# Maximum of the scores ahead of the output add and the rotation sum on VectorE, in a fused FFN, attention and FFN kernel

## The chip, the cores and the metric

One core of a Trainium2 chip runs the whole program. The metric is the device time of one execution in microseconds (us), taken as the median of several executions. The engines are TensorE (PE in the profile, with its weight loads as PEld), VectorE (DVE), ScalarE (ACT), GpSimd (POOL) and SyncE (SP, which here only issues DMAs).

## What is computed

The reference is a "macaron" block in fp32 over x of shape 2 x 1024 x 256: half a mixture-of-experts FFN, causal attention with rotary positions, and the same half FFN again.

```
x = x + 0.5 * ffn(layernorm(x))
x = x + attn(layernorm(x))
x = x + 0.5 * ffn(layernorm(x))

attn: q, k, v = x @ wq, x @ wk, x @ wv        16 heads of 128
      q, k = rope(q), rope(k)
      logits = q k^T / sqrt(128), masked causally
      probs = softmax(logits)
      out = (probs @ v) @ wo
```

The FFN has 8 experts that differ by low-rank parts, with a top-2 router; it does not matter to the change.

## The kernel before

Three stages follow each other: the first FFN, the attention, the second FFN. The change is in the attention alone.

Precision: a product of two fp32 operands is made of three TensorE matmuls in a fast fp32 form, on high and low parts (`product`, lines 1241 to 1245). So each operand has to be split: ScalarE copies the high part (`..._h`), and VectorE or GpSimd subtracts it from the original for the low part (`..._l`, the helper `low` at line 295).

Attention: heads are taken in 8 pairs. A pair has four units (2 heads x 2 sequences), a unit has 8 query tiles of 128 rows, and each tile is one **step**, so `STEPS` is 32 per pair. Step t works on tile i = t % 8 of its unit; its scores are 128 x 128(i+1) elements wide. Every engine runs its own written-out list of instructions, step by step, and semaphores join them. Work of several tiles is in flight: the tile of step t is transposed at step t + 2 (`T_LAG`), its probabilities meet the values at t + 5 (`PV_LAG`, two tiles at a time), the output projection is at t + 8 (`OUT_LAG`).

What a step does, for each engine in its order of issue:

- TensorE: `scores` of tile t; the side work (`project`, a 128 x 512 piece of q or k of the unit after, in even steps, or `values` in odd ones); `weigh` (probabilities times values, even steps); `project_out` (odd steps of the even units); `turn` (transposes of tile t - 2).
- ScalarE: copies of the transposed tile t - 3 (`pT_h`, line 768); in even steps `rope_high` (line 750), the high part of the piece of q or k of step t - 2, which waits for VectorE's sum; in odd steps `oA_h` or `oB_h` and the values' high part; then `Exp` of tile t (line 789), which waits for the maximum; in even steps `swap_halves` (lines 744 and 745, two copies), which waits for VectorE's `rope_cos`.
- VectorE: the order that is changed, below; then `pT_l` of tile t - 3; `rope_cos` (line 1110, even steps) or `value_low`; the low part of the output; reciprocals of the row sums (line 1129).
- GpSimd: the scaling of tile t - 1 by its reciprocal (line 571), `rope_sin` (line 560), the low part of the piece of step t - 2.

The three instructions that change places on VectorE are these. The **output add** (line 1162) adds a 128 x 512 tile of the output projection, which TensorE has made at step t - 1, to x; it comes in even steps, in 8 of a pair's 32 (t = 2, 4, 6, 8, 18, 20, 22, 24; in the first pair only the last four). The **rotation sum** (line 1116) ends the rotation of the piece of q or k that was projected at step t - 2; it comes in all even steps for which there is such a piece. The **maximum** (line 1173) reads the scores from PSUM in place and writes the row maximum; it is in every step.

PSUM has eight banks. Banks 0 to 3 hold scores (two for a wide tile), 4 and 5 transposes, 6 the weighed values; the side work and the output projection take banks by a fixed table, and each first waits until the bank's last user has been read:

```
MISC_BANKS = [1, 3, 7, 3, 7, 7, 7, 7]

def bank_free(bank):
    if bank in bank_user:
        kind, index = bank_user[bank]
        pe.wait_ge({"proj": proj_swapped, "v": v_ready, "o": y_added}[kind], index + 1)
```

The table is by t % 8. `y_added` is raised by the output add, `proj_swapped` by the second copy of `swap_halves`.

Of the kernel before, what the change touches and what calls it, by code (L numbers as in the profile page):

```python
# [18 lines left out]
ALU = mybir.AluOpType  # L19
# [13 lines left out]
SEQ_TILES = SEQ // P  # L33
# [52 lines left out]
T_LAG, PV_LAG, OUT_LAG = 2, 5, 8  # L86
# [30 lines left out]
def build(nc, x_in, ffn_w, expand_w, attn_w, rope_w, out):  # L117
    with ExitStack() as ctx:
        def sem(name):
            return ctx.enter_context(nc.semaphore(name))  # L120

        def sbuf(stack, name, shape, dt=F32):
            return stack.enter_context(nc.sbuf_tensor(name, shape, dt))


        x_sb = sbuf(ctx, "x_sb", [P, TILES, D])
# [10 lines left out]
        ps = ctx.enter_context(nc.psum_tensor("ps", [P, 8, 512], F32))  # L137
# [146 lines left out]
        y_done = sem("y_done")  # L284
        y_added = sem("y_added")
        stored = sem("stored")

        def need(eng, semaphore, count):

            if not isinstance(count, int) or count > 0:  # L290
                eng.wait_ge(semaphore, count)
# [9 lines left out]
        def rope_low_part(eng, index, u, k):  # L301

            eng.wait_ge(proj_high, index + 1)
            h, l = ((kT_h, kT_l), (qT_h, qT_l))[k % 2]
            cols = slice(512 * (k // 2), 512 * (k // 2) + 512)
            low(eng, l[:, u % 2, cols], rot[:, k % 2], h[:, u % 2, cols]).then_inc(proj_ready, 1)
# [44 lines left out]
        def groups_before(p, t):  # L351
            u, i = unit_of(t)
            return UNITS * UNIT_GROUPS * p + UNIT_GROUPS * u + GROUPS_AT[i]
# [4 lines left out]
        def side_work(p, t, first, last):  # L358

            if t >= STEPS:
                return None
            u, i = unit_of(t)
            k = i // 2
            if i % 2 == 0:
                if u == UNITS - 1 and last:
                    return None
                return "proj", (u + 1) % UNITS, 4 * (UNITS * p + u + 1) + k, k
            if first and u == 0:  # L370
                return "v", 0, k, k
            if u % 2 == 1:
                if u == UNITS - 1 and last:
                    return None
                return "v", (u // 2 + 1) % 2, 4 * (2 * p + u // 2 + 1) + k, k
            return None

        def misc_bank(t):

            return MISC_BANKS[t % SEQ_TILES] if t < STEPS else MISC_BANKS[-1]  # L380

        def rotation_to_end(p, t, first, last):

            if t < ROPE_LAG:
                work = None if first else side_work(p - 1, t - ROPE_LAG + STEPS, False, False)
            else:
                work = side_work(p, t - ROPE_LAG, first, last)
            return work if work and work[0] == "proj" else None
# [6 lines left out]
        def chunk_of_step(p, t, lag, first):  # L395

            tile = tile_of_step(p, t, lag, first)
            if not tile or tile[1] % 2 == 0:
                return None
            q, s = tile  # L400
            u, i = unit_of(s)
            return u, i // 2, 16 * q + 4 * u + i // 2, q, s

        def out_of_step(p, t, lag, first):

            chunk = chunk_of_step(p, t, lag, first)
            if not chunk or chunk[0] % 2 == 0:
                return None
            u, c, _, q, _ = chunk
            return u // 2, c, 4 * (2 * q + u // 2) + c, q  # L410

        def score_view(slot, i):

            n = P * (i + 1)
            if n <= 512:
                return ps[:, 2 * slot:2 * slot + 1, 0:n], 1, n
            return ps[:, 2 * slot:2 * slot + 2, 0:n // 2], 2, n // 2
# [416 lines left out]
        def _(dve):  # L834
# [278 lines left out]
            def rope_sum(index, k):  # L1113
                dve.wait_ge(proj_cos, index + 1)
                dve.wait_ge(proj_sin, index + 1)
                dve.tensor_tensor(rot[:, k % 2], rot[:, k % 2], rot_sin[:], ALU.add).then_inc(proj_rot, 1)
# [6 lines left out]
            def invert_sum(p, t, first):  # L1123

                tile = tile_of_step(p, t, 1, first)
                if tile:
                    q, s = tile
                    dve.wait_ge(exp_done, STEPS * q + s + 1)
                    dve.reciprocal(inv_sum[:, s % 4:s % 4 + 1], row_sum[:, s % 4:s % 4 + 1]).then_inc(inv_done, 1)  # L1129
# [23 lines left out]

            def attention(p, first, last):
                for t in range(STEPS + (DRAIN_STEPS if last else 0)):
                    y = out_of_step(p, t, OUT_LAG + 1, first)
                    if y:
                        b, c, index, _ = y
                        tiles = x_sb[:, SEQ_TILES * b + 2 * c:SEQ_TILES * b + 2 * c + 2, :].rearrange("p a d -> p (a d)")
                        dve.wait_ge(y_done, index + 1)  # L1160
                        need(dve, y_added, index - 3)
                        dve.tensor_tensor(tiles, ps[:, misc_bank(t - 1), :], tiles, ALU.add).then_inc(y_added, 1)
                    turn = rotation_to_end(p, t, first, last)
                    if turn:
                        rope_sum(turn[2], turn[3])
                    if t % 2 == 1:
                        invert_sum(p, t, first)
                    if t < STEPS:

                        view, a, n = score_view(t % 2, t % SEQ_TILES)  # L1170
                        dve.wait_ge(scores_done, STEPS * p + t + 1)
                        dve.nop(nofuse=True)
                        dve.tensor_tensor_reduce(out=view, in0=view,  # L1173
                                                 in1=causal[:, SEQ - a * n:].rearrange("p (a n) -> p a n", a=a),
                                                 scale=-SCALE, scalar=HUGE, op0=ALU.add, op1=ALU.min,
                                                 accum_out=neg_max[:, t % 4:t % 4 + 1]).then_inc(max_done, 1)
                    if first and t < 2:

                        rope_sum(2 + t, 2 + t)
                        rope_low_part(dve, 2 + t, 0, 2 + t)  # L1180
                    if first and t == 0:
                        layer_norm_low(2 * CHUNKS - 1, CHUNKS - 1)
                    tile = tile_of_step(p, t, T_LAG + 1, first)
                    if tile:
                        q, s = tile
                        i = s % SEQ_TILES
                        half = P * (i % 2)
                        for n, (slot, count) in enumerate(tile_groups(i)):
                            dve.wait_ge(pT_high, groups_before(q, s) + n + 1)
                            bank = T_BANK + (GROUPS_AT[i] + n) % 2  # L1190
                            low(dve, pT_l[i // 2 % 2][:, slot:slot + count, half:half + P],
                                ps[:, bank, 0:P * count].rearrange("p (a b) -> p a b", a=count),
                                pT_h[i // 2 % 2][:, slot:slot + count, half:half + P]).then_inc(pT_ready, 1)
                    side = side_work(p, t, first, last)
                    if side and side[0] == "proj":
                        rope_cos(side[2], side[3], misc_bank(t))
                    elif side:
                        value_low(side[2], side[1], side[3], misc_bank(t))
                    chunk = chunk_of_step(p, t, PV_LAG + 1, first)
                    if chunk:  # L1200
                        u, c, index, _, _ = chunk
                        h, l = ((oA_h[:, 256 * c:256 * c + 256], oA_l[:, 256 * c:256 * c + 256]) if u % 2 == 0
                                else (oB_h[:, c % 2], oB_l[:, c % 2]))
                        dve.wait_ge(o_high, index + 1)
                        low(dve, l, ps[:, PV_BANK, 0:256], h).then_inc(o_ready, 1)
                    if t % 2 == 0:
                        invert_sum(p, t, first)
                    for kind, at in PAIR_SPLITS_AT.items():
                        if t == at + 1 and (kind == "o" or not last):
                            split_pair(kind, p + (kind != "o"))  # L1210
                    if last:
                        for c in range(EARLY_NORMS):
                            norm_early(2 * CHUNKS + c, c, t - STEPS)
# [514 lines left out]
```

## Time and profile before

| | |
|---|---|
| time, median of 3 runs | 1508.43 us (1506.5 to 1511.03) |
| the profiled execution's own time | 1506.33 us |
| its span, from the first to the last instruction | 1504.2 us |
| TensorE busy | 1423.6 us, 95% of the span |
| VectorE busy | 1054.9 us, 70% |
| ScalarE busy | 906.9 us, 60% |
| GpSimd busy | 786.7 us, 52% |
| mean granted TensorE clock | 0.985 |
| share of TensorE in the chain that ended last | 84% |
| attention, first to last maximum | 283.7 to 1226.4 us |

The time is the span plus a small part around it (2.1 us in the profiled execution). The table's busy shares are averages over all three stages.

### The profile page before, as it was taken

The page shows a single profiled execution, that of the slowest core. Times are in us where ns is not written, and L with a number is a line of the kernel's source. Part 1 is how long each engine was busy: PE and PEld are TensorE (multiplying, and loading weights), DVE is VectorE, ACT ScalarE, POOL GpSimd, SP SyncE. Part 2 cuts the span into 40 slices and gives each one's busy share as a digit, 9 for nine tenths or more (in the row PEclk, how much of TensorE's full clock was granted, in tenths as well). Part 3 has the DMA queues.
Part 4 walks back from the last instruction along what each step waited for, and adds up shares of the span by engine and source line. Part 5 has one row for each costly group of instructions (what it writes and reads, how often), then busy time and mean ns, then how long its engine had stood idle before and what let it go on. Part 6 is the DMA issues. An engine that isn't in the chain of part 4 may idle for free.

```text
span 1504.2 us, 25617 instructions
## 1 busy us (share of the span) xinstructions
PE 1423.6 (95%) x8912; PEld 1267.3 (84%) x8912; DVE 1054.9 (70%) x2368; ACT 906.9 (60%) x1881; POOL 786.7 (52%) x701
## 2 busy tenths in 40 slices
PE   6899999799999999999999999999999986999997
PEld 4688887588999899899989998999899975788886
DVE  6576776777767777777677767767776785665664
ACT  3544443577767766777777667776776653544432
POOL 4656354356555555555555555555555533754542
PEclk9899999799999999999999999999999999999999
DMA  4000001000000000000000000000000020000000
GB/s 165 1 1 1 1 1 49 22 8 15 9 8 10 13 8 8 15 8 8 15 1 8 22 1 8 22 1 8 8 1 2 1 110 1 0 15 1 15 15 14
DMA packets 11406, 23.40 MB, mean 16 GB/s; under 512 B 912, under 2 KB 5008, under 8 KB 11152
## 3 DMA queue, kind: packets, MB, share of 16 engines
q1 hardware_dynamic: 11280, 21.78, 4.3%
q8 instruction: 72, 1.18, 0.3%
q14 instruction: 54, 0.44, 0.1%
HBM read 19.68 MB, written 2.10 MB: 14 GB/s over the span
## 4 chain that ended last, share of the span: by engine, by line
PE 84%; DVE 10%; issue 3%; ACT 1%; POOL 1%; DMA 0%; DVEq 0%; POOLq 0%; ACTq 0%
PE ps L1243 25%; PE ps L1245 24%; PE ps L1244 24%; PE ps L1565 9%; DVE ps L1173 2%; DVE pT_l L295 1%; DVE mixed L992 1%; DVE hid L982 1%; PE ps L1256 1%; DVE stats L842 1%; POOL um_l L295 0%; DVE xn L861 0%; DVE hid L969 0%; DVE part_sum L956 0%; DMA x_sb<-x_in 0%
## 5 line engine op out<-in xcount | busy, mean ns | idle before, releaser
L571 POOL TENSOR_SCALAR probs<-probs,inv_sum 128x128 f32<-128x128 f32 (+7 forms) x256 | 213.2, 833 | 384.6 <-DVE inv_sum L1129 384.5
L1173 DVE CUSTOM_DVE_ANT_0 ps<-ps,causal 128x128 f32<-128x128 f32 (+7 forms) x256 | 195.1, 762 | 212.2 <-PE ps L1245 210.5
L789 ACT ACTIVATE probs<-ps,neg_max 128x128 f32<-128x128 f32 (+7 forms) x256 | 189.1, 739 | 74.6 <-DVE neg_max L1173 74.5
L295 POOL TENSOR_TENSOR hid_l<-hid,hid_h 128x512 fp32r<-128x512 f32 x80 | 107.6, 1345 | 182.6 <-ACT hid_h L654 182.6
L295 DVE TENSOR_TENSOR pT_l<-ps,pT_h 128x512 fp32r<-128x512 f32 (+3 forms) x384 | 200.9, 550 | 2.2 <-ACT pT_h L768 1.9
L560 POOL TENSOR_TENSOR rot_sin<-swapped,rope 128x512 f32<-128x512 f32 x128 | 165.2, 1290 | 61.2 <-ACT swapped L745 58.4
L768 ACT ACTIVATE pT_h<-ps 128x512 fp32r<-128x512 f32 (+3 forms) x384 | 174.2, 490 | 37.8 <-PE ps L1565 35.3
L1565 PE MATMUL ps<-ident,probs 128*128 128x128 f32 x1152 | 170.5, 275 | 22.7 <-DVE pT_l L295 19.4
L1244 PE MATMUL ps<-pT_l,v_h 128*128 128x256 f32 (+1 forms) x640 | 179.7, 281 | 0.0
L1245 PE MATMUL ps<-pT_h,v_l 128*128 128x256 f32 (+1 forms) x640 | 179.5, 281 | 0.0
L1243 PE MATMUL ps<-pT_h,v_h 128*128 128x256 f32 (+1 forms) x640 | 178.3, 279 | 0.8 <-DVE oA_l L295 0.8
L1565 PEld LDWEIGHTS ps<-ident,probs 128*128 128x128 f32 x1152 | 129.0, 140 | 34.4 <-issue 28.3
L1243 PE MATMUL ps<-kT_h,qT_h 128*128 128x384 f32 (+5 forms) x384 | 151.4, 394 | 4.6 <-DVE qT_l L295 4.6
L969 DVE TENSOR_TENSOR hid<-ps,spread 128x512 f32<-128x512 f32 x80 | 55.3, 691 | 108.6 <-PE ps L1245 108.5
L1245 PE MATMUL ps<-kT_h,qT_l 128*128 128x384 f32 (+5 forms) x384 | 131.2, 342 | 0.0
L1244 PE MATMUL ps<-kT_l,qT_h 128*128 128x384 f32 (+5 forms) x384 | 131.1, 341 | 0.0
L647 ACT ACTIVATE up_act<-ps 128x512 f32<-128x512 f32 (+1 forms) x96 | 56.9, 593 | 121.0 <-PE ps L1245 121.0
L1243 PEld LDWEIGHTS ps<-pT_h,v_h 128*128 128x128 f32 x640 | 121.6, 190 | 6.7 <-DVE pT_l L295 1.4
L1244 PEld LDWEIGHTS ps<-pT_l,v_h 128*128 128x128 f32 x640 | 121.7, 190 | 5.6
L1245 PEld LDWEIGHTS ps<-pT_h,v_l 128*128 128x128 f32 x640 | 121.7, 190 | 0.0
L744 ACT ACTIVATE swapped<-ps 64x512 f32<-64x512 f32 x128 | 76.2, 595 | 67.1 <-DVE rot L1110 62.4
L654 ACT ACTIVATE hid_h<-hid 128x512 fp32r<-128x512 f32 (+1 forms) x96 | 60.4, 629 | 68.3 <-DVE hid L982 68.3
(184 smaller groups left out, 4169.0 us busy)
## 6 DMA issues: line engine op xcount, KB each, us to landing
w_raw<-attn_w SPq DMA_DIRECT2D x32, 256.0 KB, 2.6
w_in<-ffn_w SPq DMA_DIRECT2D x12, 576.0 KB, 8.7
x_sb<-x_in SPq DMA_DIRECT2D x4, 512.0 KB, 5.5
out<-x_sb SPq DMA_DIRECT2D x4, 512.0 KB, 2.9
rope<-rope_w SPq DMA_DIRECT2D x1, 1024.0 KB, 6.6
w_in<-ffn_w SPq DMA_DIRECT2D x2, 264.0 KB, 4.9
spread<-expand_w SPq DMA_DIRECT2D x2, 256.0 KB, 7.8
```

The source lines that it names most:

```text
L295: return eng.tensor_tensor(dst, src, high.bitcast(F32), ALU.subtract)
L560: pool.tensor_tensor(rot_sin[:], swapped[:], rope[:, 1, 512 * ch:512 * ch + 512], ALU.mult)\
L571: pool.tensor_scalar(probs[s % 4][:, 0:n], probs[s % 4][:, 0:n], inv_sum[:, s % 4:s % 4 + 1], 1.0, ALU.mult, ALU.mult).then_inc(probs_read ...
L654: act.activation(hid_h[0:rows, j], hid[0:rows, j], ACT.Copy).then_inc(hid_high, 1)
L744: act.activation(swapped[0:64], ps[64:128, bank, :], ACT.Copy)
L768: act.activation(pT_h[i // 2 % 2][:, slot:slot + count, half:half + P], ps[:, bank, 0:P * count].rearrange("p (a b) -> p a b", a=count), A ...
L789: act.activation(probs[t % 4][:, 0:a * n].rearrange("p (a n) -> p a n", a=a), view, ACT.Exp, bias=neg_max[:, t % 4:t % 4 + 1], scale=-1.0, ...
L1173: dve.tensor_tensor_reduce(out=view, in0=view, in1=causal[:, SEQ - a * n:].rearrange("p (a n) -> p a n", a=a), scale=-SCALE, scalar=HUGE, ...
L1243: pe.matmul(dst, w[0], x[0], start=start, stop=False, skip_group_check=skip)
L1244: pe.matmul(dst, w[0], x[1], start=False, stop=False, skip_group_check=skip)
L1245: return pe.matmul(dst, w[1], x[0], start=False, stop=stop, skip_group_check=skip)
L1565: ins = pe.transpose(ps[:, bank, P * k:P * k + P], probs[s % 4][:, P * kt:P * kt + P], ident[:])
```

## The change

In VectorE's list for one attention step, the odd steps' reciprocal and the maximum move ahead of the output add and the rotation sum. In an odd step there is neither an add nor a sum, and the reciprocal is ahead of the maximum in both versions, so the order of odd steps is the same as before. In an even step the order "add, sum, maximum" becomes "maximum, add, sum". No instruction is added or removed, and the other engines' lists are as they were.

```
             def attention(p, first, last):
                 for t in range(STEPS + (DRAIN_STEPS if last else 0)):
+                    if t % 2 == 1:
+                        invert_sum(p, t, first)
+                    if t < STEPS:
+
+                        view, a, n = score_view(t % 2, t % SEQ_TILES)
+                        dve.wait_ge(scores_done, STEPS * p + t + 1)
+                        dve.nop(nofuse=True)
+                        dve.tensor_tensor_reduce(out=view, in0=view,
...
+                                                 accum_out=neg_max[:, t % 4:t % 4 + 1]).then_inc(max_done, 1)
                     y = out_of_step(p, t, OUT_LAG + 1, first)
                     if y:
                         b, c, index, _ = y
...
                     turn = rotation_to_end(p, t, first, last)
                     if turn:
                         rope_sum(turn[2], turn[3])
-                    if t % 2 == 1:
-                        invert_sum(p, t, first)
-                    if t < STEPS:
-
-                        view, a, n = score_view(t % 2, t % SEQ_TILES)
-                        dve.wait_ge(scores_done, STEPS * p + t + 1)
-                        dve.nop(nofuse=True)
-                        dve.tensor_tensor_reduce(out=view, in0=view,
...
-                                                 accum_out=neg_max[:, t % 4:t % 4 + 1]).then_inc(max_done, 1)
                     if first and t < 2:
```

## Rows read from the trace of the kernel before

**Rows 1.** Busy time by stretch, attention: us, then each engine's busy us and instructions, clock.

```profile
580.00:730.00 150.00, 147.16 (x1028) 136.45 (x1027) 110.44 (x272) 107.83 (x240) 84.85 (x81) 1.00 0.04 12
```

**Rows 2.** Groups by form, VectorE, 430 to 1180 us: busy, mean ns | idle before.

```profile
L1173 DVE CUSTOM_DVE_ANT_0 ps<-ps,causal 128x896 f32<-128x896 f32 x25 | 27.4, 1098 | 1.5
L1173 DVE CUSTOM_DVE_ANT_0 ps<-ps,causal 128x768 f32<-128x768 f32 x25 | 24.2, 967 | 76.6 <-PE ps L1245 76.6
```

**Rows 3.** Timeline, VectorE, a step 6: start us, us, what, [idle before].

```profile
601.64 0.68 DVE L1162 TENSOR_TENSOR x_sb<-ps,x_sb 128x512 f32<-128x512 f32 x1
602.24 0.68 DVE L1116 TENSOR_TENSOR rot<-rot,rot_sin 128x512 f32<-128x512 f32 x1
603.05 1.10 DVE L1173 CUSTOM_DVE_ANT_0 ps<-ps,causal 128x896 f32<-128x896 f32 x1
...
604.06 0.69 DVE L295 TENSOR_TENSOR pT_l<-ps,pT_h 128x512 fp32r<-128x512 f32 x1
```

**Rows 4.** Timeline, TensorE, the same step: end of the scores, begin of the projection.

```profile
602.53 0.36 PE L1245 MATMUL ps<-kT_h,qT_l 128*128 128x448 f32 x1
602.74 0.39 PE L1243 MATMUL ps<-xnT_h,wq_h 128*128 128x512 f32 x1
```

**Rows 5.** Timeline, VectorE and TensorE, step 7: a wait of TensorE for VectorE.

```profile
608.18 0.89 DVE L295 TENSOR_TENSOR pT_l<-ps,pT_h 128x512 fp32r<-128x512 f32 x2
...
609.02 0.85 PE L1565 MATMUL ps<-ident,probs 128*128 128x128 f32 x6 [0.63 <-DVE pT_l L295]
```

**Rows 6.** Timeline, VectorE, a step 8 with an output add.

```profile
609.32 0.68 DVE L1162 TENSOR_TENSOR x_sb<-ps,x_sb 128x512 f32<-128x512 f32 x1
609.91 0.88 DVE L1116 TENSOR_TENSOR rot<-rot,rot_sin 128x512 f32<-128x512 f32 x1
610.72 0.29 DVE L1173 CUSTOM_DVE_ANT_0 ps<-ps,causal 128x128 f32<-128x128 f32 x1
...
610.93 1.01 DVE L295 TENSOR_TENSOR pT_l<-ps,pT_h 128x512 fp32r<-128x512 f32 x2
```

**Rows 7.** Timelines of TensorE and ScalarE, the same step 8 and its step 9.

```profile
609.87 0.28 PE L1245 MATMUL ps<-kT_h,qT_l 128*128 128x128 f32 x1
...
613.79 0.98 ACT L768 ACTIVATE pT_h<-ps 128x512 fp32r<-128x512 f32 x2
...
615.45 0.74 PE L1565 MATMUL ps<-ident,probs 128*128 128x128 f32 x5
```

**Rows 8.** Timelines of TensorE, VectorE and ScalarE, steps 14 and 15.

```profile
632.22 0.37 PE L1245 MATMUL ps<-kT_h,qT_l 128*128 128x448 f32 x1
...
632.54 0.68 DVE L1116 TENSOR_TENSOR rot<-rot,rot_sin 128x512 f32<-128x512 f32 x1
633.14 1.10 DVE L1173 CUSTOM_DVE_ANT_0 ps<-ps,causal 128x896 f32<-128x896 f32 x1
...
633.26 0.63 ACT L750 ACTIVATE kT_h<-rot 128x512 fp32r<-128x512 f32 x1 [0.32 <-DVE rot L1116]
634.33 1.01 ACT L789 ACTIVATE probs<-ps,neg_max 128x896 f32<-128x896 f32 x1 [0.44 <-DVE neg_max L1173]
...
636.08 0.59 ACT L745 ACTIVATE swapped<-ps 64x512 f32<-64x512 f32 x1
...
636.72 0.19 PEld L1243 LDWEIGHTS ps<-wv_h,xnT_h 128*128 128x128 f32 x1 [0.55 <-ACT swapped L745]
```

**Rows 9.** Timeline, TensorE, behind the values of the same step 15.

```profile
638.72 0.52 PE L1565 MATMUL ps<-ident,probs 128*128 128x128 f32 x3 [0.30 <-DVE pT_l L295]
```

**Rows 10.** Busy time by stretch: two stalls of TensorE and the clock behind each.

```profile
288.85:292.27 3.42, 1.56 (x7) 0.70 (x5) 1.57 (x3) 2.25 (x6) 1.62 (x2) 1.00 0.00 0
292.27:295.68 3.41, 3.21 (x16) 3.16 (x16) 2.82 (x9) 2.52 (x6) 0.55 (x2) 0.50 0.00 0
...
1226.26:1228.38 2.12, 0.00 (x0) 0.03 (x1) 1.98 (x5) 0.65 (x1) 1.60 (x2) 1.00 0.38 123
1228.40:1240.00 11.60, 11.43 (x98) 11.26 (x99) 10.00 (x24) 6.78 (x16) 2.46 (x2) 1.00 0.01 2
```

More of the change, by code:

```diff
@@ L1155, in attention @@
                 for t in range(STEPS + (DRAIN_STEPS if last else 0)):
+                    if t % 2 == 1:
[5 more added lines that the diff above has]
+                        dve.tensor_tensor_reduce(out=view, in0=view,
+                                                 in1=causal[:, SEQ - a * n:].rearrange("p (a n) -> p a n", a=a),
+                                                 scale=-SCALE, scalar=HUGE, op0=ALU.add, op1=ALU.min,
+                                                 accum_out=neg_max[:, t % 4:t % 4 + 1]).then_inc(max_done, 1)
                     y = out_of_step(p, t, OUT_LAG + 1, first)
@@ L1165, in attention @@
                         rope_sum(turn[2], turn[3])
-                    if t % 2 == 1:
-                        invert_sum(p, t, first)
-                    if t < STEPS:
-                        view, a, n = score_view(t % 2, t % SEQ_TILES)
-                        dve.wait_ge(scores_done, STEPS * p + t + 1)
-                        dve.nop(nofuse=True)
-                        dve.tensor_tensor_reduce(out=view, in0=view,
-                                                 in1=causal[:, SEQ - a * n:].rearrange("p (a n) -> p a n", a=a),
-                                                 scale=-SCALE, scalar=HUGE, op0=ALU.add, op1=ALU.min,
-                                                 accum_out=neg_max[:, t % 4:t % 4 + 1]).then_inc(max_done, 1)
                     if first and t < 2:
```

## The prediction

> **What bounds the kernel.** I read the busy time by stretch first. In the attention TensorE is busy for 147.16 us of 150, at the full clock (2.4 GHz), VectorE for 110.44 and ScalarE for 107.83 [rows 1]. So the attention is TensorE's own work plus 2.84 us of idle time in 150. Over the 943 us between the first and the last maximum that makes 943 / 150 x 2.84 = 18 us, an estimate of all that better timing elsewhere can give. A loss has no such limit: whatever makes TensorE wait where it does not wait now is added nearly whole. I look for that.
>
> Next I read VectorE's maximum by form, since its width tells the step. It shows 25 maxima 768 wide (i = 5) with 76.6 us of idle time ahead, and 25 of 896 (i = 6) with 1.5 us [rows 2]. The other six widths repeat this: the three of odd steps wait for the scores, over 1 us each time, the three of even steps do not. But "no idle time" has two meanings, and only the timelines tell them apart. In step 6 the add begins at 601.64 and the sum at 602.24, while the scores end at 602.53 + 0.36 = 602.89 and the maximum starts at 603.05, 0.16 us behind them [rows 3, 4]. Here add and sum fill a wait: VectorE was there 1.25 us before the scores. In step 14, where there is no add, the sum starts at 632.54 and the scores end at 632.22 + 0.37 = 632.59: they are there as VectorE comes, and the maximum at 633.14 is late by the sum [rows 8]. Of a half pair's eight even steps four are of the first kind (2, 4, 6, 8), four of the second (0, 10, 12, 14). The changed order acts on even steps only.
>
> **What the maximum gains.** In the second kind it starts earlier, in step 14 at 632.59 + 0.16 = 632.75 in place of 633.14, 0.4 us. Its reader is the exponential. But ScalarE issues `rope_high` ahead of the exponential, and `rope_high` waits for the sum, which now stands behind the maximum. Before, `rope_high` ran beside the maximum, 633.26 to 633.89, and the exponential started at 634.33 [rows 8]. After: maximum 632.75, sum one maximum later (604.06 - 603.05 = 1.01 us from start to start [rows 3]) at 633.76, ended 634.44, `rope_high` until 635.1, exponential at 635.0 (such a follower starts up to 0.1 us inside its predecessor's record). It is 0.7 us later, not earlier. So the moved maximum brings nothing forward, and I cost its gain at 0, with 18 us as the bound from the idle time. The cover that the maximum gave to `rope_high` is gone in every even step that has a sum.
>
> **A: the add in step 6.** (B and C follow.) TensorE makes an output projection at step 5 in bank 7 and projects at step 6 into bank 7 again; the table has 7 for both. So the projection of step 6 waits for `y_added`, raised by the add in VectorE's step 6. Now the add ends at 602.32, before TensorE comes, and the projection's first matmul starts at 602.74 straight behind the scores [rows 3, 4]. After, the add stands behind a maximum that itself waits for the scores of that step: maximum 603.05, add 1.01 later at 604.06, ended 0.68 later at 604.74. From the end of a VectorE instruction to the matmul that it releases takes 0.15 us: `pT_l` 608.18 + 0.69 = 608.87, transposes 609.02 [rows 5]. So the projection starts at 604.89 in place of 602.74, **2.15 us** later, with nothing for TensorE to do in between, since its list is in order and `weigh`, `turn` and the scores of step 7 stand behind. Is it given back? The next wait is 0.63 us ahead of the transposes of step 7 [rows 5], but that one hangs on the maximum of step 7, hence on the scores of step 7, which have moved by the same 2.15 us. Lower bound 2.15 - 0.63 = 1.5, upper 2.15 + 0.2; I take 2.15. It happens at t = 6 and t = 22 of seven pairs and at t = 22 of the first: 15 x 2.15 = **32.3 us**. The other adds block nothing: of steps 1 and 3 (bank 3) the add is read out at least a step before the bank's next use, and bank 7 of step 7 is next used at step 10.
>
> **B: step 8 into step 9.** The scores end at 609.87 + 0.28 = 610.15 [rows 7], the maximum starts at 610.31, the add 0.21 later (610.93 - 610.72) at 610.52, the sum 0.59 later at 611.11, `pT_l` 0.60 later at 611.71 in place of 610.93 [rows 3, 6]: 0.8 us late (1.0 if the sum is as slow as its 0.88 here). `rope_cos` moves with it, `swap_halves` hangs on `rope_cos`, and ScalarE's `pT_h` of tile 6 stands right behind the swap, so it starts at 613.79 + 0.8 = 614.59 [rows 7]. Its first copy takes some 0.6 us, until 615.19; `pT_l` follows, 0.69 long [rows 3], until 615.9, and the transposes that wait for it start 0.15 us later (A), at 616.05 in place of 615.45 [rows 7]: **0.6 us**. Bounds 0 and 0.8. Fourteen such steps (t = 24 of the first pair, 8 and 24 of six, 8 of the last): 14 x 0.6 = **8.4 us**. Steps 2 and 4 delay VectorE likewise by about 1.0 and 1.2 us, but the maxima of steps 3 and 5 have idle time ahead of them to take it (76.6 / 25 = 3.1 us a step in step 5 [rows 2]); I cost them at 0, and at 0.1 us each if that cover is short.
>
> **C: step 14 into step 15.** Here TensorE already waits for `swap_halves`, because the values of step 15 take bank 7 behind the projection of step 14. The copy ends at 636.08 + 0.59 = 636.67, the weight load is at 636.72 [rows 8]. The swap is behind the exponential, which comes 0.7 us later (above), so the values start 0.7 us later. The transposes behind them had 0.30 us of wait of their own [rows 9], which comes off: 0.4, of which the overlap of the records (TensorE's rows end up to 0.1 us inside each other) leaves 0.3. ScalarE and VectorE go into the next unit some 0.35 us later than TensorE, and its transposes of step 1 hang on the tight chain of B: 0.2 more. **0.5 us**, bounds 0.3 and 0.7. Sixteen such places (t = 15 of eight pairs, t = 31 of seven, t = 7 of the first): **8 us**. Nothing else moves: SyncE's and GpSimd's lists are the same, no DMA is issued by the moved lines, and GpSimd's scaling, which comes later with the reciprocals and the swap, is read by transposes a step or more behind it. I cost it at 0; if it lacks room for tile 7, it meets the wait of B in step 9.
>
> **Sum**: 32.3 + 8.4 + 8.0 = 48.7 us. On the profiled execution's 1506.33 us that is 1555.0. That execution lies 2.1 us below the median of the runs shown, so I name 1556.
>
> **The rivals.**
>
> *A alone, B and C absorbed.* For it: the chains of B and C are sums of small differences, each with 0.1 to 0.3 us of slack that I may have wrong. 1506.3 + 32.3 = 1538.6.
>
> *The clock falls behind A.* A stall of 1.86 us at 289 us, in a stretch in which TensorE was busy for 1.56 of 3.42 us, was followed by 3.41 us at a granted clock of 0.50 (1.2 GHz); one of 2.13 us at 1226 us was not: the clock stayed at 1.00 [rows 10]. A's stall lies between. Each such spell costs half its length, 1.7 us; 15 of them make 26 us, 1581. Against it: the dense work on both sides of A's stall resembles the second row more. The Trainium skill ("TensorE: Matmul & The Clock Gate", Part 1: The HAM clock gate) says that the throttled state is the default and that activity lifts it; by that rule a stall in dense work is the risk here, and the first of the two stalls agrees with it, the second does not show it.
>
> *Delays pile up.* B's and C's upper bounds, 14 x 0.8 + 16 x 0.7 = 22, and 0.1 us in each of 60 steps 2 and 4, 6: 1506.3 + 32.3 + 28 = 1567, up to 1575 if A's stall also upsets the steps behind it.
>
> *Not slower.* The earlier maximum lets the exponential go earlier and TensorE's idle time shrinks. The place is the exponential of the steps without an add; the price at most 18 us of gain, so 1488 if A costs nothing and 1521 with A whole. It decides only where A's stall is under 18 / 15 = 1.2 us, that is, if the bank is released 1 us earlier than worked out. Against it are both orders: the bank table and `rope_high` ahead of the exponential.
>
> **Chances.** Likeliest case (1548 to 1562) 0.6; A alone 0.13; piling up 0.13; clock 0.1; not slower 0.04. The range of 8 in 10 leaves out the clock case and the fastest: 1535 to 1570. Slower by over 0.3% (about what a measurement of this kernel can tell from no change) 0.96, within it 0.02, faster 0.02.
>
> **What would show it.** In the changed profile, a new wait of the projection of step 6 for the output add, 15 times, about 2 us each, so that each half pair of 16 steps lasts 2.15 + 0.6 + 0.5 = 3.2 us longer than now. Idle time of VectorE ahead of the maxima 128, 384, 640 and 896 wide, about 1 us in half of them. The exponentials of even steps wait for nothing on VectorE directly, since ScalarE comes from `rope_high`. The wait for `swapped` ahead of `values` over 1 us in step 15, TensorE's transposes of step 9 waiting for `pT_l`. TensorE's busy time and its matmul counts are unchanged. The prediction is wrong if the add does not gate the projection, if exponentials of even steps start earlier, or if the clock row of the attention falls below 1.00.

## The result and the profile after

| | before | changed |
|---|---|---|
| time, median of 4 runs | 1507.57 us (1506.5 to 1511.03) | 1577.02 us (1574.0 to 1579.34) |
| ratio | | 1.0448, 95% interval 1.0428 to 1.0468 |
| the profiled execution's own time | 1506.33 us | 1577.85 us |
| first maximum, last maximum | 283.7, 1226.4 us | 287.7, 1298.1 us |
| granted TensorE clock, mean | 0.985 | 0.970 |

The change costs 69 us. The forecast was 1556 us with a range of 1535 to 1570: the sign was right, the size too small, and the time is outside the range. From its first to its last maximum the attention takes 1298.1 - 287.7 = 1010.4 us in place of 942.7, so 67.7 us of the loss are there. (The first maximum is 4.0 us later too, behind an FFN that the change doesn't touch; in the runs below this start lies between 1.3 us earlier and 5.0 us later than before, which speaks for the execution and against the change as its cause.)

The next line is the busy time by stretch, to be compared with [rows 1]; the columns are the same. TensorE idles 8.57 us in 150 in place of 2.84, and the clock is below 1.00:

```profile
580.00:730.00 150.00, 141.43 (x960) 129.97 (x960) 101.90 (x246) 97.95 (x219) 75.81 (x75) 0.98 0.03 8
```

The waits in the attention, 430 to 1180 us (total, times, longest), name what is new:

```profile
ACT kT_h L750 <- DVE rot L1116: 84.0, 47, 2.9
ACT qT_h L750 <- DVE rot L1116: 58.4, 35, 2.6
...
PEld ps L1243 <- DVE x_sb L1173: 27.4, 12, 2.3
PE ps L1243 <- DVE x_sb L1173: 22.8, 12, 1.9
...
PE ps L1565 <- DVE pT_l L295: 17.9, 34, 1.0
...
PEld ps L1243 <- ACT swapped L745: 11.8, 12, 1.0
...
PE ps L1243 <- ACT swapped L745: 6.7, 12, 0.6
```

TensorE waits for `x_sb`, the output add (now line 1173), 12 times in this window for 1.9 us each: that is A, and it was nowhere before. The wait for `swapped` is C's, that for `pT_l` partly B's. ScalarE's `rope_high` waits 142 us in total for the sum, which is behind the maximum; in the same window it waited 29.8 us before.

A step 6 on VectorE and on TensorE, as in [rows 3] and [rows 4]:

```profile
624.87 1.10 DVE L1163 CUSTOM_DVE_ANT_0 ps<-ps,causal 128x896 f32<-128x896 f32 x1 [1.32 <-PE ps L1245]
...
625.88 0.69 DVE L1173 TENSOR_TENSOR x_sb<-ps,x_sb 128x512 f32<-128x512 f32 x1
626.49 0.68 DVE L1116 TENSOR_TENSOR rot<-rot,rot_sin 128x512 f32<-128x512 f32 x1
```

```profile
624.35 0.37 PE L1245 MATMUL ps<-kT_h,qT_l 128*128 128x448 f32 x1
626.62 0.50 PE L1243 MATMUL ps<-xnT_h,wq_h 128*128 128x512 f32 x1 [1.91 <-DVE x_sb L1173]
626.96 0.42 PE L1244 MATMUL ps<-xnT_l,wq_h 128*128 128x512 f32 x1
627.19 0.61 PE L1245 MATMUL ps<-xnT_h,wq_l 128*128 128x512 f32 x1
627.61 0.63 PE L1243 MATMUL ps<-xnT_h,wq_h 128*128 128x512 f32 x1
628.03 0.63 PE L1244 MATMUL ps<-xnT_l,wq_h 128*128 128x512 f32 x1
```

The first part is what the forecast drew: maximum, add 1.01 us later, projection 0.05 us behind the add's end at 626.57, after a stall of 1.91 us. The second part, the matmuls behind the stall, it did not put into its sum. From the third matmul on, starts are 0.42 us apart; in a step 6 of the same kernel that goes at full speed they are 0.23 apart:

```profile
563.84 0.50 PE L1243 MATMUL ps<-xnT_h,wq_h 128*128 128x512 f32 x1 [1.91 <-DVE x_sb L1173]
564.17 0.39 PE L1244 MATMUL ps<-xnT_l,wq_h 128*128 128x512 f32 x1
564.40 0.39 PE L1245 MATMUL ps<-xnT_h,wq_l 128*128 128x512 f32 x1
564.63 0.39 PE L1243 MATMUL ps<-xnT_h,wq_h 128*128 128x512 f32 x1
```

The busy time by stretch, with the clock as the third figure from the end, shows the difference between the two (the first three rows are one step 6, the fourth is the other):

```profile
626.62:627.20 0.58, 0.58 (x3) 0.49 (x4) 0.58 (x2) 0.00 (x0) 0.00 (x0) 1.00 0.00 0
627.20:630.61 3.41, 3.41 (x14) 3.03 (x13) 1.99 (x5) 2.37 (x5) 0.56 (x1) 0.50 0.00 0
630.61:640.00 9.39, 8.70 (x64) 7.98 (x62) 6.30 (x16) 6.01 (x14) 5.02 (x5) 1.00 0.11 28
563.84:570.00 6.16, 5.67 (x35) 4.96 (x35) 3.74 (x9) 4.30 (x9) 3.38 (x3) 1.00 0.00 0
```

Behind 11 of the 15 stalls TensorE is granted 0.50 (1.2 GHz in place of 2.4) for 3.41 us. The maxima of steps 6 and 7 price both kinds:

```profile
562.08 1.10 DVE L1163 CUSTOM_DVE_ANT_0 ps<-ps,causal 128x896 f32<-128x896 f32 x1 [1.32 <-PE ps L1245]
...
568.23 1.23 DVE L1163 CUSTOM_DVE_ANT_0 ps<-ps,causal 128x1024 f32<-128x1024 f32 x1 [1.88 <-PE ps L1245]
...
632.60 1.23 DVE L1163 CUSTOM_DVE_ANT_0 ps<-ps,causal 128x1024 f32<-128x1024 f32 x1 [2.05 <-PE ps L1245]
```

Before, the maximum of step 7 followed that of step 6 (603.05 [rows 3]) by 3.98 us:

```profile
607.03 1.23 DVE L1173 CUSTOM_DVE_ANT_0 ps<-ps,causal 128x1024 f32<-128x1024 f32 x1 [0.96 <-PE ps L1245]
```

Here it is 568.23 - 562.08 = 6.15, **2.17 us** more, where the clock stays, and 632.60 - 624.87 = 7.73, another **1.58 us** more, where it falls. A is 15 x 2.17 = 32.5 us and the low clock 11 x 1.58 = 17.4 us. (A "spell" is from here on a stretch of 3.41 us at 0.50. Each count of spells belongs to one execution, the profiled one.)

### The profile page after: what moved, and what is told of

It is laid out like the page before. It is cut to its first block, busy times and chain, and to the rows that moved or that the text cites. A ratio compares the mean times of both kernels' runs of the same rounds, so it can differ in the third digit from the quotient of the medians.

```text
span 1575.7 us, 25617 instructions
## 1 busy us (share of the span) xinstructions
PE 1446.9 (92%) x8912; PEld 1281.8 (81%) x8912; DVE 1064.2 (68%) x2368; ACT 898.3 (57%) x1881; POOL 774.8 (49%) x701
## 4 chain that ended last, share of the span: by engine, by line
PE 66%; DVE 17%; ACT 8%; issue 6%; POOL 1%; DMA 0%; DVEq 0%; ACTq 0%; POOLq 0%
PE ps L1243 20%; PE ps L1245 19%; PE ps L1244 19%; PE ps L1565 6%; DVE pT_l L295 3%; ACT swapped L744 2%; DVE rot L1116 2%; DVE ps L1163 2%; ACT swapped L745 2%; DVE rot L1110 1%; ACT probs L789 1%; ACT v_h L755 1%; ACT pT_h L768 1%; DVE v_l L295 1%; DVE mixed L992 1%
## 5 line engine op out<-in xcount | busy, mean ns | idle before, releaser
L571 POOL TENSOR_SCALAR probs<-probs,inv_sum 128x128 f32<-128x128 f32 (+7 forms) x256 | 201.2, 786 | 442.0 <-DVE inv_sum L1129 441.9
L1565 PE MATMUL ps<-ident,probs 128*128 128x128 f32 x1152 | 178.3, 281 | 32.3 <-DVE pT_l L295 27.4
L1565 PEld LDWEIGHTS ps<-ident,probs 128*128 128x128 f32 x1152 | 132.6, 143 | 47.0 <-issue 30.1
L750 ACT ACTIVATE kT_h<-rot 128x512 fp32r<-128x512 f32 x64 | 40.4, 631 | 111.6 <-DVE rot L1116 111.5
```

The costliest lines, as they stand in the source:

```text
L571: pool.tensor_scalar(probs[s % 4][:, 0:n], probs[s % 4][:, 0:n], inv_sum[:, s % 4:s % 4 + 1], 1.0, ALU.mult, ALU.mult).then_inc(probs_read ...
L1565: ins = pe.transpose(ps[:, bank, P * k:P * k + P], probs[s % 4][:, P * kt:P * kt + P], ident[:])
```

## The experiments

Each kernel's time stands beside runs of the kernel before on the same chip. "Length" is the attention from its first to its last maximum in the profile, 942.7 us before. In the edits, `maximum()`, `output_add()` and `rotation_sum()` stand for the lines of those three instructions, and guards for the ends of the loop are left out.

**The add of step 6 left ahead.**

```
-                    maximum(); output_add(); rotation_sum()
+                    if t % 8 == 6:
+                        output_add(); maximum(); rotation_sum()
+                    else:
+                        maximum(); output_add(); rotation_sum()
```

> The changed kernel, but with the output add left ahead of the maximum in the steps with t % 8 == 6 (order there: add, maximum, sum). My theory: the wait of the projection of step 6 for the bank (A) and the low clock behind it are gone together, and only the delays B (step 9) and C (steps 15 and 1) stay: 1507.6 + 14 x 0.6 + 16 x 0.5 = 1524 us, clock 1.00 all through the attention. Rival, delays in the other even steps lower the clock or pile up by themselves: some spells at 0.50 stay and the time is 1535 us or more.

Measured: 1530.9 us (1528.6 to 1534.9) beside 1508.8, ratio 1.0157 [1.0131, 1.0183]; length 965.8. One place of two instructions was worth 46 us of 69: the stalls at the projection are gone, and with them all spells at 0.50 in the stretch from 310 to 1200 us:

```profile
310.00:1200.00 890.00, 860.22 (x5967) 790.77 (x5966) 640.04 (x1552) 613.14 (x1377) 476.21 (x469) 1.00 0.03 9
```

The remaining 22 us are 6 more than B and C. Most of that is a cost that the forecast did not have, 0.24 us in each step 6, shown in the run with the sum alone, below; another 1.4 us is one spell at 1230 us, outside that stretch but inside the length, at two waits for `pT_l` of 0.95 and 1.33 us that stand close together near the end of this kernel's attention.

**The add of step 6 alone, on the kernel before.**

```
+                    if t % 8 == 6:
+                        rotation_sum(); maximum(); output_add()
+                    else:
                         output_add(); rotation_sum(); maximum()
```

> The kernel before, with one thing moved: in the steps with t % 8 == 6 the output add goes behind the maximum (order: sum, maximum, add). My theory: TensorE stalls 1.9 us ahead of the projection in 15 steps, which is 15 x 2.15 = 32 us, and behind about 11 of the stalls it runs 3.4 us at a granted clock of 0.50, some 1.6 us each: 1507.6 + 32 + 17 = 1557 us. Rival, the low clock needs the other delays as well (stall alone): 1540 us and a clock of 1.00 in the attention. Rival, the stall is given back where nothing else is late: under 1535 us.

Measured: 1544.0 us (1542.8 to 1545.3), ratio 1.0234 [1.0215, 1.0252]; length 979.7, 37.0 more. The stall is whole by itself, in 15 places, and nothing is given back:

```profile
PE ps L1257 <- DVE x_sb L1165: 24.8, 13, 1.9
```

But only 3 of the 15 stalls are followed by a spell: 15 x 2.17 + 3 x 1.58 = 37.3 us. My 11 spells were a wrong guess, and so was 1557. Equal stalls, an unequal number of spells.

**The stall filled with work of no use.**

```
+                    if t < STEPS and t % 8 == 6 and out_of_step(p, t, OUT_LAG + 1, first):
+                        pe.wait_ge(exp_done, STEPS * p + t)
+                        for _ in range(8):
+                            pe.matmul(ps[:, 2 * ((t + 1) % 2), :], xnT_h[:, 0, 0:P],
+                                      xnT_h[:, 0, 0:512], start=True, stop=True)
                     side(p, t, first, last)
```

> The changed kernel, with 8 extra matmuls of 512 columns (results overwritten by the next scores) issued by TensorE ahead of the projection of each step 6 that has to wait for an output add; they fill the 1.9 us stall with work of no use (8 x 0.23 = 1.84 us). If the low clock comes from the stall: no spell at 0.50 is left in the attention, the projections still start at the same moment behind the add, and the time falls from 1577 to about 1577 - 11 x 1.6 = 1560 us although TensorE does 120 matmuls more. If the clock has another cause (the work of the step itself, delays elsewhere): the spells stay and the time is 1577 us or more.

Measured: 1557.2 us (1556.8 to 1559.7), ratio 1.0328 [1.0308, 1.0349]; length 992.8. With 120 matmuls more the kernel is 20 us faster than the changed one. The clock over the attention, the changed kernel first, then this one:

```profile
310.00:1200.00 890.00, 835.41 (x5704) 768.46 (x5703) 612.96 (x1483) 587.05 (x1315) 455.64 (x447) 0.98 0.03 9
```

```profile
310.00:1200.00 890.00, 857.88 (x5896) 787.35 (x5894) 622.61 (x1504) 596.29 (x1339) 462.58 (x455) 1.00 0.03 9
```

No spell is left in that stretch. The rest of the loss is as it was (the maxima of steps 6 and 7 are again 2.16 us further apart than before, and those of the other steps stand as in the changed kernel), so this kernel measures what the change costs without the clock: 992.8 - 942.7 = 50.1 us. And 1010.4 - 992.8 = 17.6 us is what the clock adds, against 11 x 1.58 = 17.4. The Trainium skill ("TensorE: Matmul & The Clock Gate", Part 1: The HAM clock gate) has it that activity releases the throttle. These runs agree as far as they go: with activity of no use in the stall, the clock does not fall behind it.

**Half of the filling.** The same with `range(4)`.

> The changed kernel with 4 extra matmuls ahead of the projection of step 6 in place of 8: the stall shrinks from 1.9 to about 1.0 us. If a stall of 1.0 us in dense work is short enough not to lower the clock, the time is that of the run with 8, 1557 us, and no spell at 0.50 is in the attention. If it still does in some places: 1557 us and 1.6 us more for each spell.

Measured: 1559.5 us (1557.1 to 1561.9), ratio 1.0338 [1.031, 1.0365]; length 993.0. The stalls are 1.00 us long and no spell follows any of the 15. A stall of 1.00 us leaves the clock alone here; one of 1.90 us may not.

**The same stalls at another spacing.** The kernel with the add of step 6 alone, and

```
+                    if t < STEPS and t % 16 == 12:
+                        pe.wait_ge(exp_done, STEPS * p + t)
+                        for _ in range(4): ...      the same matmuls
                     side(p, t, first, last)
```

> The kernel before with the add of step 6 alone behind the maximum (1544 us, 15 stalls of 1.90 us, but only 3 spells at 0.50 in its profile, against 11 in the changed kernel), and 4 matmuls of no use ahead of the projection in the steps with t % 16 == 12. They add dense work, 16 x 0.92 = 15 us, and move the stalls to the spacing of 62.6 us that the changed kernel would have without its spells. If the place of a stall in time decides whether the clock falls behind it, the number of spells goes up to 8 or more: 1544 + 15 + 5 x 1.6 = 1567 us or more. If the short waits of steps 9 and 15 in the changed kernel are what adds to its stalls, the number stays near 3: 1559 us.

Measured: 1571.9 us (1567.9 to 1580.1), ratio 1.0429 [1.0377, 1.0481]; length 1009.2. In the profile 7 of 15 stalls are followed by a spell, in place of 3, though neither the stalls nor the work next to them have changed. The filler costs 1.45 us a half pair, not 0.92: 15 x 2.17 + 16 x 1.45 + 7 x 1.58 = 66.8 against a measured 66.5. That points to the place of a stall in time as what decides, and speaks against the short waits of steps 9 and 15, since this kernel has those of the kernel before and not those of the changed one. It is 7 and not the 8 or more that I had set as the mark, and the filler is itself a second change. The number is not fixed by the kernel either: the four executions lie 12 us apart, those at 1574.2 and 1580.1 us with a mean granted clock of 0.975, those at 1567.9 and 1569.6 with 0.980.

The traces say what it is about the place. In every trace here, all falls and rises of the granted clock lie on one regular beat of time, whose offset from the kernel's first instruction differs from trace to trace. In the four kernels with the full stall (the changed one, this one, the one with the add of step 6 alone, and the one with the add alone, below) there are 60 stalls of 1.90 us. With the beat taken 0.04 us early, 24 of them lie whole between two beats, and these are the 24 that a spell follows; 36 are cut by a beat, and none of them is followed by one. Of the 15 stalls of 1.00 us, 10 lie between two beats, and no spell follows. This was found in the traces afterwards; no run was made to foretell which stalls it would be.

**The sum alone behind the maximum.**

```
-                    output_add(); rotation_sum(); maximum()
+                    output_add(); maximum(); rotation_sum()
```

> The kernel before with the rotation sum alone moved behind the maximum (order in every even step: add, maximum, sum). My theory: no bank is held longer, so no stall in step 6 and no low clock; the exponential comes later behind rope_high, the swap of step 14 with it, C stays (16 x 0.5 = 8 us), and B shrinks to 0 to 0.2 us in 14 places: 1516 to 1519 us. Rival, C needs the moved add of the same half pair: within 3 us of the kernel before. Rival, the earlier maximum is worth something: faster than before.

Measured: 1526.8 us over its ordinary executions (1525.8 to 1529.1), ratio 1.0118 [1.01, 1.0136]: twice what I expected. (One execution, the profiled one, took 4870 us and is left out. In it TensorE's matmuls took two to three times as long as elsewhere and the other engines' instructions as long as ever; why is open, and it did not come again.) So I ran it again for a profile.

> The same kernel as the rotation-sum run before (sum alone behind the maximum), for a profile of it; its time was 1526.8 us, 18 us over the kernel before, against 8 to 11 that I expected. My theory now: the first seven or eight microseconds are the swap of step 14 as expected (0.3 a half pair); the rest are transposes of steps 6 and 14 that wait for the low part of tile t - 3, which the sum delays by 0.6 us (0.2 each), and a step 9 that is as late as in the changed kernel (0.6). Rival: spells at a clock of 0.50 in the attention.

Measured: 1528.4 us, length 960.1, 17.4 more; no spell. The list of TensorE's waits, 430 to 1180 us:

```profile
PE ps L1252 <- ACT swapped L745: 14.8, 25, 0.6
...
PEld ps L1252 <- ACT swapped L745: 11.7, 12, 1.0
...
PE ps L1574 <- DVE pT_l L295: 7.1, 25, 0.4
```

TensorE waits for the swap in 25 places, in place of 12 in the changed kernel: in step 15 (C), and also in step 7, where the output projection takes bank 7 behind the projection of step 6. There it stands in place of the wait for `pT_l` of 0.63 us [rows 5], which is gone, so it costs nothing; in the changed kernel, behind A's stall, there is no such wait. The maxima show the net cost of a half pair: 0.24 us between the maxima of steps 6 and 7, 0.34 by step 11 (B), 0.22 by step 15, 0.3 by step 2 of the next. That is 1.1, and 16 x 1.1 = 17.6. The 0.24 and the 0.22 are the transposes of steps 6 and 14, whose second group waits for `pT_l` of tile t - 3, which the sum delays. The same can be read in the changed kernel, in its step 14 (VectorE, ScalarE, TensorE; compare [rows 8]):

```profile
658.87 1.10 DVE L1163 CUSTOM_DVE_ANT_0 ps<-ps,causal 128x896 f32<-128x896 f32 x1
...
659.88 0.69 DVE L1116 TENSOR_TENSOR rot<-rot,rot_sin 128x512 f32<-128x512 f32 x1
660.49 0.68 DVE L295 TENSOR_TENSOR pT_l<-ps,pT_h 128x512 fp32r<-128x512 f32 x1
```

```profile
660.60 0.63 ACT L750 ACTIVATE kT_h<-rot 128x512 fp32r<-128x512 f32 x1 [1.53 <-DVE rot L1116]
661.14 0.99 ACT L789 ACTIVATE probs<-ps,neg_max 128x896 f32<-128x896 f32 x1
...
662.85 0.59 ACT L745 ACTIVATE swapped<-ps 64x512 f32<-64x512 f32 x1
```

```profile
660.62 0.94 PE L1565 MATMUL ps<-ident,probs 128*128 128x128 f32 x5
...
663.50 0.39 PE L1243 MATMUL ps<-wv_h,xnT_h 128*128 128x256 f32 x1 [0.54 <-ACT swapped L745]
```

The maximum is at 658.87, and the exponential that reads it starts at 661.14, since `rope_high` of 0.63 us stands between: the chain of the forecast. The five transposes take 0.94 us, because the last waits for the `pT_l` that ends at 661.17; before, the five took 0.73 us. The values stall 0.54 us behind the swap, where they stalled 0.13 before.

That longer wait of step 15 adds nothing where it stands. Behind it the transposes' own 0.30 us [rows 9] is gone, and the first scores of step 0 start 3.12 us behind the last matmul of the scores of step 15 in both kernels (639.32 - 636.20 before, 665.68 - 662.56 after). It shows in step 1 of the next unit: values, their high and low parts and with them VectorE's list come later, the swap of step 0 too, and the transposes of step 1 now wait. The last score matmul and the transposes of that step, before and after:

```profile
643.54 0.28 PE L1245 MATMUL ps<-kT_h,qT_l 128*128 128x256 f32 x1
...
645.27 1.06 PE L1565 MATMUL ps<-ident,probs 128*128 128x128 f32 x8
```

```profile
669.90 0.28 PE L1245 MATMUL ps<-kT_h,qT_l 128*128 128x256 f32 x1
...
671.94 1.06 PE L1565 MATMUL ps<-ident,probs 128*128 128x128 f32 x8 [0.32 <-DVE pT_l L295]
```

The distance grows from 1.73 to 2.04 us. That is the 0.3 of the list above (0.33 by the scores of step 2).

**The add alone behind the maximum, in all even steps.**

```
-                    output_add(); rotation_sum(); maximum()
+                    rotation_sum(); maximum(); output_add()
```

> The counterpart of the run with the sum alone behind the maximum: the kernel before with the output add alone behind the maximum, in all even steps (order: sum, maximum, add). My theory: A in full, 32 us, with some spells at 0.50 (3 to 11, 1.6 us each), part of B (0.2 to 0.35 in 14 places) and nothing of C, since sum, rope_high and exponential stand as before: 1545 to 1562 us. Rival, C is not tied to the sum: another 8 us.

Measured: 1548.4 us (1548.4 to 1551.4), ratio 1.0264 [1.0244, 1.0284]; length 980.2, 37.5 more, with 3 spells. A is whole, C absent, and B almost absent: 37.5 - 32.5 - 3 x 1.58 = 0.3 us. Add and sum alone cost 32.8 and 17.4 us without the clock, together 50.2, and the changed kernel without the clock 50.1. But B is not a sum of parts that each show it in full: 0.34 with the sum alone, near nothing with the add alone, 0.59 with both.

**`rope_high` behind the exponential.** The kernel with the add of step 6 left ahead, and on ScalarE

```
-                    if turn: rope_high(...)
                     ...
                     Exp of step t
+                    if turn: rope_high(...)
```

> The kernel in which the add of step 6 stays ahead and all else is as changed (1530.9 us), and on ScalarE rope_high moved behind the exponential of the same step, so that the exponential can follow the earlier maximum. My theory: the delay of the exponential behind rope_high is what makes the swap of step 14 late, so the part of C at step 15 goes (0.3 a half pair, 5 us), while the transposes of steps 6 and 14 (0.22 each) and step 9 (0.6), which hang on the sum, stay: 1525 to 1527 us. Rival, the earlier maximum is worth something once ScalarE lets it through: 1509 us or less. Rival, rope_high is harmless where it stands: 1531 us.

Measured: 1519.5 us (1518.9 to 1521.6), ratio 1.0076 [1.0051, 1.0101]; length 956.4, 9.3 less than without it. ScalarE's timeline of a step 14:

```profile
579.37 1.01 ACT L790 ACTIVATE probs<-ps,neg_max 128x896 f32<-128x896 f32 x1 [0.99 <-DVE neg_max L1181]
...
580.37 0.62 ACT L750 ACTIVATE kT_h<-rot 128x512 fp32r<-128x512 f32 x1
581.11 0.60 ACT L744 ACTIVATE swapped<-ps 64x512 f32<-64x512 f32 x1
```

The exponential now follows the maximum, and `rope_high` fits ahead of the swap. The wait for the swap at step 15 is back at 0.10 us, and with it C's part at step 1 is gone: there the half pair is even 0.14 us shorter than before (0.3 longer without this edit). Of the 9.3 us, 1.4 are the one spell that the kernel without the edit had; the rest is mostly this difference, 16 times. The transposes of steps 6 and 14 and B stay, so it does not beat the kernel before.

**`rope_high` behind the exponential, VectorE as before.** ScalarE's edit alone.

> The kernel before with rope_high behind the exponential on ScalarE in all even steps and VectorE's order as it was. This isolates ScalarE's order. The maximum is no earlier, so the exponential gains nothing, and rope_high, which ran beside the maximum, now stands ahead of the swap: in steps without slack the swap is up to 0.5 us later. My theory: slower by 16 x 0.3 = 5 us, 1512 us. Rival: the swap waits for rope_cos anyway and nothing changes, 1507 us.

Measured: 1524.2 us (1521.7 to 1528.6), ratio 1.01 [1.0077, 1.0123]; length 955.4. It costs 14 us where I expected 5. So of the two pairs of orders each alone is worse: with the sum ahead of the maximum, `rope_high` belongs ahead of the exponential, where it runs beside the maximum.

**Two attempts to beat the kernel before.** The first changes both orders in the three kinds of steps in which nothing is delayed by it:

```
+                    if t % 16 in (0, 10, 12):
+                        maximum(); rotation_sum()       ScalarE: Exp, then rope_high
+                    else:
                         output_add(); rotation_sum(); maximum()
```

> An attempt to beat the kernel before: its VectorE order in all steps but t % 16 = 0, 10 and 12 (no output add, scores already there, no transposes that the delay of the low part reaches); in those three the maximum goes ahead of the sum and on ScalarE rope_high goes behind the exponential. The run with rope_high behind the exponential gained 0.14 us a half pair on the kernel before around step 0. My theory: 16 x 0.15 = 2 us faster, at the edge of what can be measured, 1505 to 1507 us. Rival, without the other delays there is nothing to gain: the same as before. Rival, rope_high behind the exponential makes the swap late: 1510 us or more.

Measured over five rounds: 1507.6 us (1503.1 to 1510.7) beside 1510.1, ratio 0.9986 [0.9973, 0.9999]; length 941.0, 1.7 us less. It has the best ratio of all the kernels with an edit, but its gain of 0.14% is under the 0.3% that I named as the resolution, so it counts as the same; the profile's 1.7 us agree with the sign, and 16 x 0.11 us at step 1 are as much.

The second takes the low parts ahead of the maximum in step 7, where TensorE waits for them [rows 5]:

```
                     output_add(); rotation_sum()
-                    maximum()
+                    if t % 8 != 7: maximum()
                     ...                             the low parts of tile t - 3
+                    if t % 8 == 7: maximum()
```

> Another attempt: the kernel before, with the low parts of tile t - 3 ahead of the maximum in the steps with t % 8 == 7, where TensorE waits 0.63 or 0.30 us for them behind the maximum. If the wait can be had: 15 x 0.6 + 16 x 0.3 = up to 14 us faster, 1494 us. My theory: the maximum and the exponential of step 7 come 1 us later, and with them the copies and low parts that the transposes of step 9 wait for, so most of it is given back: 1503 to 1510 us. Rival, the delay is larger than the gain: 1512 us or more.

Measured: 1519.3 us (1516.6 to 1519.7), ratio 1.0059 [1.004, 1.0078]; length 953.5. More than was gained is given back: the waits of 0.63 us in step 7 and 0.30 in step 15 are gone, and two of 0.74 to 0.78 us (steps 1 and 9) and one of 0.28 (step 8), for later low parts, stand in each half pair. TensorE's wait for `pT_l` goes from 12.5 us to

```profile
PE ps L1577 <- DVE pT_l L295: 22.7, 38, 0.8
```

## Why the forecast was right in direction and wrong in size

- **"So the moved maximum brings nothing forward."** Right. `rope_high` waits for the sum 142 us in 750, and the exponential follows it. The run with `rope_high` moved shows that the order was the reason; even then the gain is 0.14 us a half pair. (Step 8 was counted among the steps whose maximum is not late. In [rows 6, 7] it is: scores end at 610.15, maximum at 610.72. B had this right, so no term hangs on it.)
- **A, 15 x 2.15 = 32.3 us.** Right: 15 x 2.17 = 32.5. The add of step 6 alone lengthens the attention by 37.0 us, of which three spells are 3 x 1.58 = 4.7, which leaves 32.3: nothing is given back at step 7. Two small errors cancel in it. The projection starts 0.05 us and not 0.15 behind the add, and its second matmul starts 0.33 us behind the first (564.17 - 563.84) in place of 0.22 (602.96 - 602.74 before).
- **B, 14 x 0.6 = 8.4 us.** Right: 0.59 by the maxima of step 11. The changed kernel's step 9, ScalarE, VectorE and TensorE, has the chain as it was drawn in the forecast (swap, copy, low part, transposes; compare [rows 7]), with a wait at the end:

```profile
639.53 0.59 ACT L745 ACTIVATE swapped<-ps 64x512 f32<-64x512 f32 x1
640.15 0.98 ACT L768 ACTIVATE pT_h<-ps 128x512 fp32r<-128x512 f32 x2
```

```profile
640.78 1.16 DVE L295 TENSOR_TENSOR pT_l<-ps,pT_h 128x512 fp32r<-128x512 f32 x2 [0.45 <-ACT pT_h L768]
```

```profile
641.62 1.06 PE L1565 MATMUL ps<-ident,probs 128*128 128x128 f32 x8 [0.51 <-DVE pT_l L295]
```

- **C, 16 x 0.5 = 8 us.** Right in size: 0.22 us by step 15 and 0.33 at step 1, 16 x 0.55 = 8.8. The parts were drawn as 0.3 and 0.2. The values do start 0.65 us later against the scores of step 14 (0.7 was foretold), but 0.22 of that is there before the swap is waited for: it is the second group of the transposes of step 14, which the forecast costed at nothing. What is left comes off again ahead of step 0. With the swap no longer late (`rope_high` behind the exponential) the 0.23 of step 14 stays and only the part at step 1 goes. The twin of that group, in step 6, lies under A; only without A does it show, with 0.24 us.
- **Steps 2 and 4, at 0.** Right: they add 0.0 to 0.1 us each.
- **The sum, 48.7 us.** The kernel with the stalls filled measures it, 50.1 us. So of the 22.8 us between 1555.0 and the profiled 1577.85, 1.4 are the sum's, 17.6 the clock's, and 4.0 the later first maximum.
- **"The clock falls behind A", chance 0.1, priced at 26 us if in all 15 places.** This is the step that failed. It happened, in 11 places, for 17.4 us. The price of one spell, 1.7 us, was right (1.58); the sum should have held it. The forecast had one stall of 1.86 us with a spell behind it and one of 2.13 us without [rows 10]. Two such rows are one for and one against, which bears out a chance near a half for each stall, hence an expected 7 or so of 15, some 12 us, and a range up to 1555 + 26. I gave it 0.1 because "the dense work on both sides of A's stall resembles the second row more", and that resemblance decides nothing: all 15 stalls of the changed kernel have the same dense work around them, and 11 fall one way, 4 the other. Nor was the second row a property of its stall. The same stall of 2.13 us stands behind the last maximum in 12 of the 13 traces (the 4870 us execution left out); a spell follows it in 3, the clock falls 0.2 us before its end in 3, and it stays at 1.00 in 6. The number of 11 is the luck of one execution; an expected number was all that could be put into the sum.

## What to carry to other kernels

Ask of every step that is moved behind a wait which buffer it frees and who takes that buffer next: here one 0.68 us add, moved behind one maximum, freed a PSUM bank 2.4 us later against the scores (0.57 us ahead of their end before, 1.85 behind it after), which held TensorE for 2.17 us. With the low clock behind it, that was 50 of 68 us. An engine that waits in either order has two different kinds of slack, work that fills the wait and work that is late; only the end of the producer against the start of the consumer tells them apart. And where TensorE is the bound, price a new stall of about 2 us with the low clock that may follow it, as an expected number of spells and not as all or nothing.

## What the runs showed of the hardware

Stalls of TensorE of equal length (1.90 to 1.91 us) in equal work were followed by 3.41 us at a granted clock of 0.50 in 11 of 15 cases, 3 of 15, 3 of 15 and 7 of 15, by kernel; stalls of 1.00 us in none of 15. A spell costs 1.58 us. Which stalls it was went by where they lay against a regular beat on which, in each trace, all changes of the clock fall: 24 of the 24 that lay whole between two beats, none of the 36 that a beat cut. Matmuls of no use in a stall are faster than an empty stall: 120 of them saved 20 us.
